# Two layers in one kernel: the table's product two projections later, and a new order of small steps in the first attention group

## The reference, cut to what matters

```python
# layer 0, 1024 tokens (2 x 512) of 256 channels
h = rmsnorm(layernorm(x));  proj = h @ in_proj_w     # gate | ssm | dt | B | C
y = ssd_scan(conv+silu(ssm), B, C, dt) * silu(gate);  s = layernorm(x) + y @ out_proj_w
router = layernorm(x) @ gate_w.T;  top 2 of 8 experts # mixture of experts, I = 704
m = sum_e weight_e * ((silu(xt @ fc1_e.T) * (xt @ fc2_e.T)) @ proj_e.T)
x = x + silu(m) * s
# layer 1, on the layernorm of x: 32 query heads, 8 key/value heads of 64, causal
q, k = rope(xn @ Wq.T), rope(xn @ Wk.T);  v = xn @ Wv.T
o = softmax(q @ k.T / 8, causal) @ v @ Wo.T
g = silu(alpha * (sign(norm2 * gamma + beta) @ sign(W - mean(W)).T + bias))
x = x + o * g
```

## Time and profile before

| | us |
|---|---|
| median of the runs (743.49 to 743.97) | 743.55 |
| the profiled execution's own time | 744.36 |
| its span, first to last instruction | 742.6 |
| PE busy | 690.8 (93%) |
| DVE busy | 514.1 (69%) |
| ACT busy | 440.8 (59%) |
| POOL busy | 392.5 (53%) |

### The profile page before, as it was taken

One profiled execution on the slowest core, in us unless ns is written; L12 is line 12 of the kernel. 1 busy time (PEld: TensorE's weight loads), 2 busy tenths in 40 slices (PEclk: granted clock), 3 DMA queues, 4 the chain that ended last, 5 costly groups with the idle time before them and its releaser, 6 DMA issues.

```text
span 742.6 us, 13492 instructions
## 1 busy us (share of the span) xinstructions
PE 690.8 (93%) x4483; PEld 600.2 (81%) x4483; DVE 514.1 (69%) x1076; ACT 440.8 (59%) x1075; POOL 392.5 (53%) x442
## 2 busy tenths in 40 slices
PE   5989999999999999899879999999999999999995
PEld 3877999998999998687668888888888888887874
DVE  7584456535333245897878879888888888887775
ACT  4435442441441442548776787778887888777782
POOL 1414343433224332236665797778877788777550
PEclk9989999999999999999999999999999999999999
DMA  8165887887877756236433332442324323242011
GB/s 287 51 199 177 262 259 253 263 262 224 252 238 225 244 171 163 43 98 201 121 105 80 95 78 65 100 93 70 94 65 107 87 66 91 50 121 58 1 29 57
DMA packets 108453, 102.25 MB, mean 138 GB/s; under 512 B 51104, under 2 KB 78688, under 8 KB 108256
## 3 DMA queue, kind: packets, MB, share of 16 engines
q1 hardware_dynamic: 106272, 95.62, 44.9%
q0 software_dynamic: 2112, 5.77, 2.4%
HBM read 69.24 MB, written 11.14 MB: 108 GB/s over the span
## 4 chain that ended last, share of the span: by engine, by line
PE 63%; DVE 21%; ACT 6%; issue 6%; POOL 2%; DMA 1%; SPq 1%; DVEq 0%; ACTq 0%
PE bank L1735 14%; PE bank L1769 8%; PE bank L1570 6%; PE bank L1908 5%; DVE p_lo L1083 3%; PE bank L1875 3%; DVE o_rest L1092 3%; PE bank L1574 3%; DVE nmax L1074 3%; PE bank L1876 3%; PE bank L1575 3%; PE bank L1576 3%; DVE q_mix L1040 2%; DVE q_mix L1041 2%; PE bank L1919 2%
## 5 line engine op out<-in xcount | busy, mean ns | idle before, releaser
L1532 POOL TENSOR_TENSOR prob<-prob,rinv 128x128 f32<-128x128 f32 (+3 forms) x256 | 176.5, 722 | 90.3 <-DVE rinv L1079 90.3
L1334 ACT ACTIVATE prob<-bank,nmax 128x512 f32<-128x512 f32 (+3 forms) x256 | 133.1, 525 | 41.5 <-DVE nmax L1074 34.2
L1083 DVE TENSOR_TENSOR p_lo<-bank,p_hi 128x512 fp32r<-128x512 f32 x160 | 109.6, 685 | 57.4 <-ACT p_hi L1341 55.2
L1341 ACT ACTIVATE p_hi<-bank 128x512 fp32r<-128x512 f32 x160 | 95.3, 595 | 45.9 <-PE bank L1570 45.0
L1735 PE MATMUL bank<-xgT,wm 128*128 128x128 f32 x920 | 111.3, 275 | 0.5 <-ACT xgT L1246 0.5
L1735 PEld LDWEIGHTS bank<-xgT,wm 128*128 128x128 f32 x920 | 108.7, 192 | 3.3 <-issue 1.4
L1875 PE MATMUL bank<-kT,qT 128*128 128x512 f32 (+3 forms) x256 | 83.7, 333 | 19.5 <-ACT prob L1334 15.1
L1570 PE MATMUL bank<-cst,prob 128*128 128x128 f32 x640 | 96.6, 274 | 0.8 <-DVE p_lo L1083 0.5
L1074 DVE TENSOR_REDUCE nmax<-bank 128x1 f32<-128x512 f32 (+2 forms) x192 | 91.4, 503 | 3.2 <-PE bank L1878 3.1
L1908 PE MATMUL bank<-p_lo,v_parts 128*128 128x256 f32 (+3 forms) x288 | 91.8, 342 | 0.2
L1505 POOL DMA_INDIRECT y_rows<-y_row,to_row x21 | 22.7, 1082 | 108.9 <-DVE y_row L943 86.4
(11 more groups left out here) (323 smaller groups left out, 1540.1 us busy)
## 6 DMA issues: line engine op xcount, KB each, us to landing
wm<-in_w_moe SPq DMA_DIRECT2D x23, 1280.0 KB
wm<-in_w_moe SPq DMA_DIRECT2D x23, 640.0 KB, 5.7
qT<-q_hi SPq DMA_DIRECT2D x124, 64.0 KB, 2.0
qT<-q_lo SPq DMA_DIRECT2D x124, 64.0 KB, 2.0
wo_twice<-wo_hi SPq DMA_DIRECT2D x32, 128.0 KB, 2.5
k_exp<-k_rows SPq DMA_DIRECT2D x56, 64.0 KB, 2.0
wtl<-in_w_moe_tail SPq DMA_DIRECT2D x46, 64.0 KB
y_rows<-gate SPq DMA_DIRECT2D x1, 2048.0 KB, 14.0
```

The source lines that it names most:

```text
L1083: TT(p_lo[:, b_, :], bank[2 + b_ % 2][:, :], p_hi[:, b_, :].bitcast(F32), ALU.subtract).then_inc(plo_done, 1)
L1334: ins = actv(prob[:, i % 2, h, POFF[j]:POFF[j] + (j + 1) * P], bk[:, at:at + (j + 1) * P], ACT.Exp, bias=nmax[:, i % 2, h, j:j + 1], accum ...
L1341: actv(p_hi[:, b_, :], bank[2 + b_ % 2][:, :], ACT.Copy).then_inc(phi_done, 1)
L1532: ins = GT(seg, seg, rinv[:, i % 2, k, j:j + 1].to_broadcast([P, (j + 1) * P]), ALU.mult)
```

## The change

Four edits, all in the order of work; no instruction is added or left out.

1. `TABLE_AFTER` goes from 12 to 14: two more projections (12 matmuls) stand ahead of the table's product.
2. The eight scalings F leave the list and stand, as a block, between the last value copy and the two credits.
3. In the first group's list KW goes from step 2 to step 1; the rotations of the second batch's keys go from (12, 8.2) and (13, 8.2) to (11, 3.4) and (12, 3.4); the lower part of pair 2's queries goes from (11, 3.3) to (12, 8.3), so behind them.
4. On SP's queue `double_wo(0)` goes ahead of `store_k(1, 1)`.

```diff
-BETWEEN, RANK_AFTER, TABLE_AFTER = 3, 6, 12
+BETWEEN, RANK_AFTER, TABLE_AFTER = 3, 6, 14
@@ half_first(i, n)
-        return z + [(n + 2, 8.1, "qa", i, 0), (n + 3, 4.5, "h", i, 0), (n + 4, 3.3, "ql", i, 0)]
+        return z + [(n + 2, 8.1, "qa", i, 0), (n + 3, 4.5, "h", i, 0), (n + (5 if i == 2 else 4), 8.3 if i == 2 else 3.3, "ql", i, 0)]
@@ kind == "first"
-        ready += [(2, 7, "KW", 0, 0), (3, 0, "VQ", 0, 0)] + half_first(2, 7) + half_first(3, 13)
+        ready += [(1, 7, "KW", 0, 0), (3, 0, "VQ", 0, 0)] + half_first(2, 7) + half_first(3, 13)
         for b in range(BATCH):
             n = 4 + 7 * b
             for k in range(2):
-                ready += [(n + k, 8.2, "Kq", b, k), (n + k + 1, 8.2, "Kr", b, k), (n + k + 4, 6.2, "Ka", b, k)]
-        ready += [(8 + t, 8.95, "F", t, 0) for t in range(NT)]
+                ready += [(n + k, 8.2, "Kq", b, k), (n + k + 4, 6.2, "Ka", b, k)]
+                ready += [(n + k, 3.4, "Kr", b, k) if b else (n + k + 1, 8.2, "Kr", b, k)]
@@ SP
             move_q(1, 0)
+            double_wo(0)
             store_k(1, 1)
             spread_k(1, 1)
             load_v(1, 1)
-            double_wo(0)
             load_wo(1)
@@ ACT, attend
-                    elif op == "F":
-                        act.wait_ge(second_ready, 1)
-                        actv(xn2[:, i, :], xn1[:, i, :], ACT.Copy, scale=sv[:, 5, i:i + 1]).then_inc(h_ready, 1)
@@ ACT, ahead of the first group
             for t in range(2, TB):
                 copy_v(t)
+            act.wait_ge(second_ready, 1)
+            for t in range(NT):
+                actv(xn2[:, t, :], xn1[:, t, :], ACT.Copy, scale=sv[:, 5, t:t + 1]).then_inc(h_ready, 1)
             act.sem_inc(exp_done, 2)
```

## The result

| | before | after |
|---|---|---|
| median of the runs, us | 743.76 (743.49 to 745.95, 4 runs) | 734.37 (734.23 to 735.71, 4 runs) |
| the profiled execution's own time | 744.36 | 734.23 |
| its span | 742.6 | 732.4 |

The ratio is 0.9868, with a 95% interval of 0.985 to 0.9886: faster by 9.4 us in the medians and by 9.8 (8.5 to 11.2) by the ratio. Forecast were 734.4 us and a gain of 9.2, counted from 743.55, the median of the first three of the four runs.

A forecast was written before the change was run, and what follows sets the result against it. PE (93% busy) was taken to bound the kernel, with DVE nearly without a pause in the first attention group. Terms -5.5 - 0.4 - 0.5 - 1.4 - 1.4 = -9.2 us from 743.55 gave 734.4 us, range 732.0 to 740.0.

The forecast's parts named there:

- Edit 1, -5.5: Stage 1, table's product: PE's wait of 2.35 us goes, and 3.2 us of slow clock with it; -5.5 us.
- The term for the clock: Stage 1, table and projections behind it: without the pause the clock stays at 2.4 GHz; 3.2 us, bounds 0 and 3.3.
- rival 1: Stage 1, table: small matmuls, not the pause, lower the clock, so the fall comes again; 737.5 us, chance 0.14.
- Edit 2, -0.4: ACT before the first scores: scalings hide in idle time, one leaves a later chain; -0.4 us, bounds 0 and -0.5.
- the bound of +1.4: First scores: up to 1.4 us late if PE's credits are given only when the block of scalings has ended.
- Edit 3, key weights, -0.5: First group: PE's 1.37 us wait for lower key weights goes, POOL's division is met next; -0.5 us.
- Edit 3, rotation, -1.4: First group: PE's 2.29 us wait for the rotation goes, but only DVE's idle time can be lost; -1.4 us.
- Edit 4, -1.4: First group: PE's 1.38 us wait for the doubled output weights goes, SP's cover hides later key stores; -1.4 us.
- a term that the forecast had only as a bound: First group, around the rotation wait: PE's slow clock in this stretch, 1.5 us, counted only in the lower bound.
- Rival 2: First group: DVE or POOL hold it whatever the order, the group's edits give 0 to 1 us; 737.5 us, chance 0.12.
- Rival 3: Start of stage 2: something else than the table's operands decides it, only edits 3 and 4 count; 739.8 us, chance 0.05.
- Rival 4: First group: DVE meets the second rotation before a scores' maximum and both engines stand; slower, 745.6 us, chance 0.03.

The follow-up runs named there:

- e2: Kernel before, table in its old place, ten matmuls whose output nobody reads filling PE's wait for the table's operands; 740.64 us, ratio 0.9939.
- e1: Kernel before with only the table's product moved two projections later (TABLE_AFTER 14); 738.69 us, ratio 0.9915.
- e3: Kernel before with the table's product two projections later and its last operand delayed on DVE, so the pause stays; 744.53 us, ratio 0.9986.
- e5: Kernel before with only the eight scalings moved as a block ahead of the two credits; 744.29 us, ratio 0.9998.
- e6: Kernel before with only the split of the second key weights (KW) a step earlier; 744.7 us, ratio 1.0012.
- e7: Kernel before with only the second keys' rotations earlier and the queries' lower part behind them; 743.93 us, ratio 0.9998.
- e4: Kernel before with only the doubled output weights ahead of the key store on SP's queue; 743.76 us, ratio 0.9985.
- b2: Kernel after, with the first group's queries' addition behind the next step's scores' maximum instead of ahead of it; 731.64 us, ratio 0.9826 to the kernel before.
- e12: Kernel before with the scalings, first group's list and doubled output weights changed, but the table's product in its old place; 740.68 us, ratio 0.995.
- b1: Kernel after, with the four sign copies of the second token half at steps 9, 10, 15 and 16; 734.52 us, ratio 0.9863 to the kernel before.
- b3: Kernel after with the changes of b1 and b2 together; 731.52 us, ratio 0.9825 to the kernel before.

## Why the prediction was right

**Edit 1, -5.5: right in mechanism and near in size.** The wait of 2.35 us went, and the fall of the clock with it. The term for the clock was taken as 3.2; e2 measures it by itself as 3.2 (66.63 to 63.44). The whole is 6.0 us in the profile and 6.3 (5.0 to 7.6) in e1's runs. Of the half microsecond more, 0.25 is no gain: this execution comes to the same point, the last matmul of the twelfth projection, 0.25 us earlier (45.90 against 46.15), DVE with it (48.04 against 48.30), which no edit touches. Counted from that point the kernel after and e1 both give 5.8. The fetch went out at 54.88 (forecast 55.1) and held nothing up. The step that I could only assume, pause rather than small matmuls, is what e2 and e3 show: rival 1 is out. What I added to rival 1, that the case could hold in some runs and not in others, came true: in all eight profiles with a pause ahead of the table the clock fell (at 50.1 to 53.3) and in none of the six without, but in nine of 147 runs with the pause the mean clock leaves no room for the whole fall. What the Trainium skill says in "TensorE: Matmul & The Clock Gate", Part 1, of a monitor that runs freely agrees with these nine runs, and with the moment of the fall, which shifts by 1.7 us between kernels whose table starts within 0.6 us.

**Edit 2, -0.4: near in size.** By e5's ratio it isn't told from zero; at the same mean clock it is 0.5 to 0.8 us, by step 20 0.3. The first scores start 0.23 us behind the product before them, at 324.10, while the block of scalings ends at 324.75: the credits behind the block were handed on ahead of its end, and the bound of +1.4 did not come. The Trainium skill, "TensorE: Matmul & The Clock Gate", Part 1, has ACT's queue eight deep and strictly first in, first out; the trace agrees that the sequencer runs ahead of its engine.

**Edit 3, key weights, -0.5: right at step 20 (-0.56).** The forecast named POOL's division as the next wait, and it is there (0.65 us in e6, 0.66 in the kernel after). That the gain can be given back at wo_twice without edit 4, as in e6's profile, I had not said; the sum had edit 4 in it, so it came out right.

**Edit 3, rotation, -1.4: the step that failed.** Alone it gives nothing (e7). I took DVE's idle time in the earlier trace rows as what could be lost, 1.48 us in all; less than half of it (0.65 in e4) is there when PE's clock is at full rate, and the 0.35 us that the reorder saved on DVE the addition took back by lasting 2.04 us instead of 1.72. Two things were wrong: the idle time was read from a stretch that a slow clock had stretched, and DVE's instructions were taken to last as long in the new order as in the old, where the addition ends by POOL's division and not by its own start. That a wait of PE is worth no more than DVE's idle time behind it no run contradicts. What limits there is one place, the maximum of the scores behind the addition, and b2 shows it. The reading that PE has three single waits in this group was incomplete, too: four more, 0.72 to 1.36 us, were there, three of them for the exponentials, and the forecast new wait for these was an old one that grew.

**Edit 4, -1.4: right.** The wait is gone and e4's step 25 is 1.1 to 1.7 us earlier; the runs say 1.1 with an interval from 2.5 to -0.2, and 1.1 at the same mean clock. The 1.38 us that I took for the wait is one draw of 0.86 to 1.48. SP's cover sufficed: the key stores followed without a wait that PE saw.

**The sum.** Forecast for the group were 3.7 us, measured 3.7 (2.5 to 4.8) by e12. That this agrees so well is luck. With the rotation at zero the forecast's parts are 2.3; against 53.7 and 69.1 to 69.7, step 20 is 1.35 us earlier and step 25 2.4 to 3.1, and runs of the same mean clock differ by 2.8 to 3.0. Of the 1.35, e6 has 0.56 and e5 0.3; the last half microsecond appears only in the combination, and no run assigns it. The rest up to 3.7 comes with a term that the forecast had only as a bound (1.5 us for PE's slow clock in this stretch): the slow stretch near 365 us is in three of the seven profiles with a wait of 2.0 to 2.3 us for v_all and in none of the seven without, and low mean clocks are in 37 of 117 runs with it and in none of 30 without. That the wait brings this stretch is likely by these counts; no run filled that wait to show it.

**The rivals.** Rival 2 (DVE or POOL hold the group) is half right: not DVE's sum of work but its order, and POOL's division beside it, hold it; for the rotation alone it came true, and b2 breaks it without taking one instruction away. Rival 3 is out (stage 2 began 6.0 us earlier); its 739.8 us is the sum with edits 2, 3 and 4, not with 3 and 4 alone as written, which would be 740.3. Rival 4 named the right danger, a scores' maximum that stands behind other work on DVE, at the wrong place: it was there before, behind the addition.

## What to carry to other kernels

A pause of TensorE can cost more behind it than in it: 2.35 us of waiting brought 3.2 us of half clock, so look at the granted clock behind each wait and count both, and note that filler products in the gap bought the second part back (e2). When a wait of the bounding engine goes and the time stays, go to the next engine that is without a pause and ask which of its instructions somebody waits for; putting that one ahead of the one that nobody waits for yet gave more (2.7 us) than removing the wait. Look at POOL's rows beside a DVE operation whose length changes with its place. Read idle times from a stretch at full clock, compare runs of the same mean clock where gains are near 1 us, and test edits of one region together as well as alone.

## What the runs showed that was not expected

- The slow stretches of the clock come and go between executions of the same order of work. The one near 306 us is in e1, b1 and b2, not in after, e2 or b3, and in none of the eight that had the slow clock at the table; with it step 0 is 0.7 to 0.9 us later, counted from the last projection (264.7 to 264.9 against 263.95). The one near 365 is worth about 1 us. Where they lie is known for the profiled execution of each kernel alone; for the other runs only the mean clock is on record.
- The 128x1024 addition on DVE took 1.21 to 2.05 us, and the whole difference goes with how long POOL's running operation went on as it started (the rows are with e7). It seems to go the other way too: POOL's 128x512 addition (L1521), which starts while DVE's runs, took 2.25 us there and 1.28 us where it started before DVE's.
- 69-column f32 products of the table: 0.11 us each at full clock (3.68 us for 32).
